# GpSimd copies a chunk's gather indices in the middle of the chunk before, in a graph-attention and mixture-of-experts kernel

## What is computed

```python
h = (x_flat @ W_gat).reshape(M, HEADS, NUM_EXPERTS)
src = jnp.concatenate([edge_index[0], loops])
dst = jnp.concatenate([edge_index[1], loops])
e = jax.nn.leaky_relu(a_src[src] + a_dst[dst], negative_slope=0.2)
e_max = jax.ops.segment_max(e, dst, num_segments=M)
ee = jnp.exp(e - e_max[dst])
denom = jax.ops.segment_sum(ee, dst, num_segments=M)
msg = h[src] * alpha[:, :, None]
agg = jax.ops.segment_sum(msg, dst, num_segments=M)
```

## Time and profile before

| | us |
|---|---|
| three runs | 8624.76, 8624.89, 8629.44 |
| median | 8624.89 |
| span of the profiled execution | 8970.5 |
| of it up to the chunk stage | about 2181 |
| chunk stage | about 6110 |
| behind it | about 680 |

### The profile page before, as it was taken

One profiled execution on the slowest core, in us unless ns is written; L12 is line 12 of the kernel. 1 busy time (PEld: TensorE's weight loads), 2 busy tenths in 40 slices (PEclk: granted clock), 3 DMA queues, 4 the chain that ended last, 5 costly groups with the idle time before them and its releaser, 6 DMA issues.

```text
span 8970.5 us, 47299 instructions
## 1 busy us (share of the span) xinstructions
PE 3224.9 (36%) x14234; PEld 1538.7 (17%) x14234; DVE 3779.2 (42%) x3541; ACT 1782.2 (20%) x2553; POOL 5015.0 (56%) x4952
## 2 busy tenths in 40 slices
PE   3556766664122222222222222222222222200477
PEld 2334444342010000000001000000010000000122
DVE  5998888886223222322232223221111111111599
ACT  1345554442111111111111111111111111100000
POOL 0111111113777777777777777776666666675541
PEclk8778888887565666565665665656565656555555
DMA  1000000001122221212222212111111111111355
GB/s 46 23 25 29 30 31 31 23 30 51 43 57 62 56 61 49 66 48 63 52 64 54 61 49 66 48 48 29 34 29 36 33 32 32 30 21 18 118 175 174
DMA packets 284764, 455.16 MB, mean 51 GB/s; under 512 B 121214, under 2 KB 204382, under 8 KB 262366
## 3 DMA queue, kind: packets, MB, share of 16 engines
q1 hardware_dynamic: 134760, 395.02, 12.1%
q0 software_dynamic: 147648, 56.99, 6.4%
q10 hardware_dynamic: 2208, 1.05, 0.0%
HBM read 231.29 MB, written 221.42 MB: 50 GB/s over the span
## 4 chain that ended last, share of the span: by engine, by line
POOL 49%; issue 19%; another core or an unknown queue 3%; PE 3%; DVE 2%; DMA 0%; POOLq 0%; ACT 0%; DVEq 0%; ACTq 0%; SPq 0%
POOL gath L1277 49%; PE bank L1519 3%; DVE yo L1492 1%; DVE fin L1497 0%; POOL idx L1272 0%; DMA gate_rows<-gate_dram 0%; DVE s L1453 0%; POOL first L1707 0%; DVE sc L1450 0%; DVE sc L1447 0%; DVE sc L1445 0%; DVE sc L1462 0%; DVE key_b L573 0%; DVE sc L1463 0%
## 5 line engine op out<-in xcount | busy, mean ns | idle before, releaser
L1277 POOL DMA_INDIRECT gath<-node_rows,idx x4352 | 4396.1, 1010 | 1666.9 <-issue 1358.9
L1239 PE MATMUL bank<-xm,w_s 128*128 128x512 f32 x1024 | 665.1, 798 | 3241.2 <-ACT scratch_i L1256 2889.0
L1182 DVE TENSOR_SCALAR scratch_i<-bank,b_s 128x512 f32<-128x512 f32 x256 | 192.0, 750 | 3385.1 <-remote 1898.6
L1246 PE MATMUL bank<-scratch_i,w_s 128*128 128x512 f32 x1024 | 796.0, 936 | 1024.6 <-issue 656.5
L1239 PEld LDWEIGHTS bank<-xm,w_s 128*128 128x128 f32 x1024 | 248.5, 262 | 3682.9 <-ACT scratch_i L1256 3087.8
L1259 ACT ACTIVATE bank<-diff 128x256 f32<-128x256 f32 x68 | 26.3, 387 | 4272.4 <-DVE diff L1212 2140.7
L1035 POOL TENSOR_TENSOR scratch_i<-xc,dst_f 128x480 f32<-128x480 f32 x64 | 85.2, 1332 | 1303.8 <-ACT dst_f L952 1303.8
L1195 DVE TENSOR_TENSOR adst_in<-bank,gath 128x256 f32<-128x256 f32 x68 | 53.4, 785 | 1263.7 <-DMA gath<-node_rows,idx 890.8
L1246 PEld LDWEIGHTS bank<-scratch_i,w_s 128*128 128x128 f32 x1024 | 277.2, 291 | 1503.9 <-issue 1349.0
L1519 PE MATMUL bank<-gate_rows,choose 4*128 4x512 f32 x512 | 449.7, 1066 | 105.4 <-DVE yo L1492 68.7
L1256 ACT ACTIVATE scratch_i<-bank,b_s 128x512 f32<-128x512 f32 x512 | 344.7, 686 | 574.2 <-remote 252.0
(11 more groups left out here) (215 smaller groups left out, 5694.9 us busy)
## 6 DMA issues: line engine op xcount, KB each, us to landing
gath<-node_rows,idx POOLq DMA_INDIRECT x4352
y_dram<-scratch_i SPq DMA_DIRECT2D x64, 1024.0 KB
yo<-y_dram SPq DMA_DIRECT2D x64, 1024.0 KB
edge_rows<-rows SPq DMA_DIRECT2D x68, 768.0 KB
line<-moved SPq DMA_DIRECT2D x21, 2048.0 KB
moved<-line SPq DMA_DIRECT2D x20, 2048.0 KB
scratch_i<-in_x SPq DMA_DIRECT2D x64, 256.0 KB, 2.7
x_dram<-x SPq DMA_DIRECT2D x64, 256.0 KB, 2.2
```

The lines of the kernel that those rows point to most:

```text
L1182: e.tensor_scalar(yt[par][:, ex, :], bank[:, 2 + b, :], b2_s[:, ex:ex + 1], None, ALU.add).then_inc(y_evac[b], 1)
L1239: e.matmul(bank[:, k % 2, :], w1_s[:, k // 2, P * (k % 2):P * (k % 2) + P], xm[par][:, :], start=True, stop=True).then_inc(up_full, 1)
L1246: m = e.matmul(bank[:, 2 + b, :], w2_s[:, ex, k, :], hid[:, 2 * ex + k, :], start=k == 0, stop=k == 1)
L1277: e.indirect_dma_start(gath[par][:, j, :], None, node_rows, bass.IndirectOffsetOnAxis(ap=idx[par][:, j:j + 1].bitcast(U32), axis=0)).then_ ...
```

## The change

The copy of the indices becomes a function, `copy_indices`. It is called once for chunk 0 ahead of the loop, and from then on in the middle of each chunk: between the 32nd and the 33rd gather of chunk c GpSimd waits for `edge_used` to show that chunk c-1 is done and copies the indices of chunk c+1 into the other half of `idx`. At the start of a chunk it waits for `edge_used` and `idx_ready` as before. The loop has 33 turns, and the last two chunks are written out behind it, because the last one has no next one.

```diff
-        def chunk_pool(e, c, par, i, col):
+        def copy_indices(e, c, par):
+
+            e.tensor_copy(idx[par][:, :], keys[1][:, bass.ds(c * U, U)].bitcast(I32)).then_inc(idx_ready, 1)
+
+        def chunk_pool(e, c, par, ahead=True):
 
             e.wait_ge(edge_used, c - 1 + OPEN)
-            e.tensor_copy(idx[par][:, :], keys[1][:, bass.ds(col, U)].bitcast(I32)).then_inc(idx_ready, 1)
             e.wait_ge(idx_ready, c + 1 + OPEN)
 
             e.sem_inc(idx_taken, 1)
             for j in range(U):
+                if ahead and j == U // 2:
+
+                    e.wait_ge(edge_used, c + OPEN)
+                    copy_indices(e, c + 1, 1 - par)
                 e.indirect_dma_start(gath[par][:, j, :], None, node_rows,
...
+            copy_indices(e, 0, 0)
-            with e.Fori(0, (EPIECE + TPIECE) // 2) as i:
+            with e.Fori(0, (EPIECE + TPIECE) // 2 - 1) as i:
                 for par in range(2):
-                    chunk_pool(e, i * 2 + par, par, i, (i * 2 + par) * U)
+                    chunk_pool(e, i * 2 + par, par)
+            for par in range(2):
+                chunk_pool(e, EPIECE + TPIECE - 2 + par, par, par == 0)
```

## The result

The changed kernel takes **8570.78 us** (median; 8569.95 to 8572.22), before 8624.83 in the same comparison (the predicted time was worked out from 8624.89, the median of three runs). The ratio is 0.9937, with an interval of 0.9923 to 0.9951: 54 us less, where 34 were forecast. The time lies just inside the range, at its fast end.

The account below looks back on a forecast made before the run. GpSimd's gathers were taken as the path: 50.9 us saved at boundaries less 16.8 for the copy in the middle gives 34 off, 8624.9 to 8591 us; range 8570 to 8630.

Parts of the forecast that it names:

- What bounds the kernel: Chunk stage: it lasts as long as GpSimd takes to send off 68 x 64 gathers, one per 1.25 us.
- The long pauses: Some chunk boundaries: 31 pauses, worth about 300 us, were read as belonging only to the profiled execution.
- Rival 4: Long pauses are real and sit on the wait for the copy's semaphore, which the change removes: 8290 us; 3%.
- The boundary term: Between chunks: copy and its wait leave, the gap falls from 1.06 to 0.30 us, saving 67 x 0.76 = 50.9 us.
- Rival 2: Chunk boundary keeps its 0.76 us because the remaining waits empty the queue: 8642, or 8676 with a cold middle; 7%.
- The copy in the middle: Between gathers 32 and 33: the copy adds 0.25 us per chunk, 67 x 0.25 = 16.8 us.
- The lower bound: Middle of a chunk: the copy costs nothing if it fits into the 0.30 us before any gather; 8574 us.
- Rival 1: Middle of a chunk: the copy costs as much as at the boundary, 0.76 us only changing place: 8625 us; 15%.
- half of the upper bound: Middle copy at half of the 0.76 us upper bound: slow end of the forecast family, about 8608 us.
- The moved wait: GpSimd's wait for DVE to finish chunk c-1, now in mid-chunk c: 16 us to spare, so no cost.
- What DVE does to the gathers: DVE's placement steps stretch three gathers early in a chunk, away from the copy; nothing was added to the sum.
- Rival 3: Placement steps catch the middle copy, 20 chunks losing up to 4.7 us each: 8685 us; 3%.

Follow-up runs that it names:

- second profile of before: The kernel before, unchanged, profiled once more: 8629.25 us plain, ratio 1.0.
- second experiment: The changed kernel with GpSimd waiting for its own index copy right behind it in the middle of each chunk: 8619.71 us, ratio 0.9989.

## Why the prediction was right, and where its sum was short

**What bounds the kernel** was right: the gathers on GpSimd are the path, and what left the gaps came off the time one for one (52 us in the stage, 54 in the plain runs).

**The long pauses** were read as belonging to the profiled execution, argued from the 346 us between span and median. The second profile of before shows it: 8621.3 us without them. Rival 4, which took them as real, is out; its 8290 lies 281 us under the measured time.

**The boundary term**, 67 x 0.76 = 50.9 us, was right: 1.06 to 0.30 at all 67. The cover named for it, the lead of the instruction stream over the engine, held; the boundary's 0.30 us, and the 0.41 of the copy with a lead placed there, show that the waits and the semaphore increment that stay cost nothing. Rival 2 is out.

**The copy in the middle** is the step that failed in size. The forecast took 0.25 us between the bounds of nothing and 0.76, by adding the copy to a full pause of 0.30. It is 0.41 - 0.30 = 0.11 us: the pause behind a copy is 0.16. 67 x 0.11 = 7 us, not 17. The row that the estimate rested on, a gather 0.30 us behind a stretched gather, says only how long a pause follows a gather; behind a copy it is 0.16. The lower bound's reason, that the copy may run in the pause, was half true. Rival 1, a copy as dear as before, needs the wait: that is the 1.06 us of the second experiment. The prediction's 8608, "half of the upper bound", does not follow from its own terms: half of 0.76 at 67 places gives 8574 + 25 = 8599.

**The moved wait** at no cost was right, and the copy behind 4 gathers shows the edge: where the 16 us to spare are spent, 5.4 us of idle time per chunk appear.

**What DVE does to the gathers** was put at nothing, and this is the missing term. The placement step starts at nearly the same time after a chunk's last gather in both kernels, behind DVE's own work on that chunk: 4113.25 - 4099.82 = 13.43 us in the second profile of before, 4095.96 - 4082.53 = 13.43 in the one after (13.3 to 13.5 in all 20 chunks of either). Here are the first two operations of the step with the gather that they stretch, in each kernel; first DVE and POOL of before:

```profile
4113.25 4.69 DVE L1110 CUSTOM_DVE_ANT_0 key_a<-key_a,moved 128x8704 uint16<-128x8704 uint16 x1
4117.97 2.43 DVE L1115 TENSOR_SCALAR moved<-key_a 128x4352 int32<-128x4352 int32 x1
```

```profile
4112.25 0.94 POOL L1277 DMA_INDIRECT gath<-node_rows,idx  x1 [0.30 <-issue]
4113.49 7.02 POOL L1277 DMA_INDIRECT gath<-node_rows,idx  x1 [0.30 <-issue]
```

and then of after:

```profile
4095.96 4.69 DVE L1110 CUSTOM_DVE_ANT_0 key_a<-key_a,moved 128x8704 uint16<-128x8704 uint16 x1
4100.69 2.43 DVE L1115 TENSOR_SCALAR moved<-key_a 128x4352 int32<-128x4352 int32 x1
```

```profile
4095.41 0.94 POOL L1284 DMA_INDIRECT gath<-node_rows,idx  x1 [0.30 <-issue]
4096.66 6.57 POOL L1284 DMA_INDIRECT gath<-node_rows,idx  x1 [0.30 <-issue]
```

The stretched gather ends at the same distance from the step's start in both (4120.51 - 4113.25 = 7.26 and 4103.23 - 4095.96 = 7.27). What differs is how many gathers were sent off before: (4113.49 - 4100.90) / 1.25, 10 of that chunk before, (4096.66 - 4082.84) / 1.25, 11 after. It is so in all 20 chunks: the stretched gather is the 11th before and the 12th after, and it begins 0.24 to 0.27 us behind the step's start before, 0.69 to 0.71 after. The shorter boundary lets a whole further gather of 1.25 us slip in ahead of the stop, so these chunks gain about 0.5 us more than the 0.76 of the boundary; seen from the gather, it is stretched to 6.57 and not 7.02. 20 x 0.45 = 9 us, about the 8.5 of the groups (whose sums hold other changes of a few us too: 4387.0 in the copy with a lead at the boundary, whose steps meet the 12th gather as well). The second experiment keeps this gain with the wait put back, and with the placement steps moved it is gone; so it is shown, and for the forecast it is luck: where the stops fell was not in its sum.

Rival 3, a copy caught by these steps, did not come about in the change; where one was caught, with the steps moved, it took the place of a stretched gather, which the rival's 94 us left out.

The sum, mended: 50.9 - 7 + 9 = 53 us, beside 52 in the stage and 54 in the plain times.

**The range** held the median by under a us (one of the four runs, 8569.95, lies below it), since its lower end rested on the free copy alone; two terms were off by about 10 us each, both to the same side. That it held is luck. The phase of the stops could have been worked out from the earlier trace rows: the step starts 4145.62 - 4132.29 = 13.33 us after the last gather's end; with a boundary of 1.06 us the 11th gather begins 13.56 us after it, behind the step's start, with one of 0.30 at 12.80, ahead of it. The prediction named the stretched gathers and looked only whether a copy would meet them, not whether the gathers would meet them at another point.

## What to carry to other kernels

Here GpSimd's wait for its own copy cost 0.65 us of gap each time (1.06 against 0.41). So put such work ahead of its use, as far as the tiles allow, and the wait is met before it is read; then look at the waits that the work itself needs, which at 4 gathers from the boundary cost more than all that was gained. Before a profile is priced, compare its span with the plain times, and take another where they differ. Where one engine's stops come at fixed times, a shift of the other engine can be worth whole instructions, more or less than the gap that was saved: here one gather more per stop, in 20 chunks.

## What had not been expected of the hardware

- One profiled execution of a kernel was 346 us longer than its plain runs, with pauses of 7 to 12 us at 33 of 67 boundaries and expert results 11 us apart; eleven other profiles, of the same and of nearly the same kernels, show none of these pauses. Up to chunk 42 they stand only ahead of even chunks, where a turn of the loop begins, and from there on at nearly every boundary. What caused them is open.
- A gather begins 0.30 us behind a gather, but 0.16 behind a copy that it need not wait for, 0.81 behind one that it waits for, and 0.45 behind a copy that had itself waited for DVE (the copy behind 4 gathers). What these times consist of is not shown.
- DVE's first two placement operations, 4.69 and 2.43 us with 0.03 us between them, hold a gather as one stop: it ends 7.3 us after the start of the first, 0.11 after the end of the second. The third operation also follows in 0.03 us, yet the gather ends 0.08 us after its start; why it gets through there is not shown.
